# Filler matmuls in the attention layer of a two-layer kernel: out of the loop bodies, and one in each vacant side slot of the last body

## The reference, cut to what matters

```python
# x: (16, 512, 128) float32; 16 heads of 8
x = L0_attn_x
xn = _layernorm(x)
q, k, v = heads(xn, Wq, bq), heads(xn, Wk, bk), heads(xn, Wv, bv)
attn = softmax(q @ k.T * scale * (0.5 + 0.5 * resolve_level))
s = (attn @ v) @ Wp.T + bp
g = _silu(ffn(xn))              # silu(xn @ wg.T) * (xn @ wu.T), then @ wd.T
x = x + s * g                   # layer 0, the one that the change touches
xn = _layernorm(x)
x = x + long_convolution(xn) * _silu(top2_experts(xn))   # layer 1
```

## Time and profile before

| | |
|---|---|
| three timed runs, median (lowest, highest) | 1589.7 us (1583.72 to 1591.99) |
| the profiled execution: time | 1592.2 us |
| the profiled execution: span, first to last instruction | 1590.4 us |
| mean granted TensorE clock | 0.924 |
| PE, DVE, ACT, POOL busy, share of the span | 82%, 65%, 55%, 35% |
| layer 0's last values matmuls end | 1010.1 us |
| a loop body | 58.2 us |

### The profile page before, as it was taken

One profiled execution on the slowest core, in us unless ns is written; L12 is line 12 of the kernel. 1 busy time (PEld: TensorE's weight loads), 2 busy tenths in 40 slices (PEclk: granted clock), 3 DMA queues, 4 the chain that ended last, 5 costly groups with the idle time before them and its releaser, 6 DMA issues. The chain is left out here.

```text
span 1590.4 us, 30375 instructions
## 1 busy us (share of the span) xinstructions
PE 1304.3 (82%) x8202; PEld 676.7 (43%) x8202; DVE 1031.1 (65%) x2496; ACT 869.9 (55%) x1682; POOL 553.7 (35%) x543
## 2 busy tenths in 40 slices
PE   5888998998998998998998898364676389999970
PEld 2433433433433333333343332133343278888860
DVE  1777877877877877877877781054556345545447
ACT  0277776776777777777676775212233144444432
POOL 2122232232232332332332221236555434445440
PEclk9999999999999999999999997555888789999995
DMA  6322202212212212211221300026988422222229
GB/s 225 105 71 107 103 33 88 102 52 67 102 53 66 102 53 70 98 57 66 100 82 39 107 11 13 13 76 229 283 271 269 146 61 68 67 67 69 67 59 317
DMA packets 109858, 160.12 MB, mean 101 GB/s; under 512 B 17489, under 2 KB 47761, under 8 KB 109394
## 3 DMA queue, kind: packets, MB, share of 16 engines
q1 hardware_dynamic: 100242, 141.14, 27.7%
q0 software_dynamic: 8448, 17.58, 3.2%
q10 hardware_dynamic: 1088, 0.54, 0.1%
HBM read 104.20 MB, written 49.77 MB: 97 GB/s over the span
## 5 line engine op out<-in xcount | busy, mean ns | idle before, releaser
L447 DVE TENSOR_REDUCE row_max<-ps_max 128x2 f32<-128x1024 f32 x512 | 623.0, 1221 | 187.5 <-PE ps_max L632 185.0
L599 ACT ACTIVATE probs<-ps_exp 128x512 f32<-128x512 f32 x1024 | 559.1, 602 | 266.2 <-PE ps_exp L632 260.5
L632 PE MATMUL ps_exp<-q_op,k_op 32*128 32x512 f32 x1024 | 320.3, 503 | 22.3 <-ACT probs L599 22.3
L632 PEld LDWEIGHTS ps_exp<-q_op,k_op 32*128 32x128 f32 x1024 | 139.2, 184 | 366.1 <-ACT probs L599 302.8
L712 PE MATMUL ps_y<-probs,v_aug 128*32 128x512 f32 x2048 | 279.7, 619 | 1.2 <-ACT probs L599 1.2
L632 PE MATMUL ps_max<-k_op,q_op 32*128 32x512 f32 x1024 | 253.0, 495 | 2.9 <-DMA k_op<-k_parts_scratch 2.2
L1475 ACT ACTIVATE hidden<-ps_h,b 128x256 f32<-128x256 f32 x268 | 118.6, 473 | 148.1 <-PE ps_h L1452 148.1
L1518 POOL DMA_INDIRECT y_scratch<-result,goes_to x134 | 128.3, 958 | 144.8 <-DVE result L1503 128.4
L1371 POOL DMA_INDIRECT sorted_scratch<-rows,place x128 | 123.5, 965 | 106.8 <-DVE place L1279 69.8
L351 POOL TENSOR_TENSOR rstd<-var_eps,minus_half 128x4 f32<-128x4 f32 x32 | 32.4, 1013 | 318.3 <-DVE var_eps L442 318.3
L1459 PE MATMUL ps_o<-w,hidden 128*128 128x128 f32 x1072 | 132.2, 277 | 0.0
(11 more groups left out here) (160 smaller groups left out, 1471.3 us busy)
## 6 DMA issues: line engine op xcount, KB each, us to landing
toep<-k_pad_scratch SPq DMA_DIRECT2D x32, 1024.0 KB
q_op<-q_parts_scratch SPq DMA_DIRECT2D x16, 1024.0 KB, 5.7
k_op<-k_parts_scratch SPq DMA_DIRECT2D x16, 1024.0 KB, 8.5
unit_rows<-sorted_scratch SPq DMA_DIRECT2D x136, 66.0 KB
q_parts_scratch<-q_hi SPq DMA_DIRECT2D x16, 512.0 KB, 3.1
k_parts_scratch<-k_hi SPq DMA_DIRECT2D x16, 512.0 KB, 2.8
q_parts_scratch<-q_lo SPq DMA_DIRECT2D x16, 256.0 KB, 2.4
k_parts_scratch<-k_lo SPq DMA_DIRECT2D x16, 256.0 KB, 2.1
```

What stands on the lines that cost most here:

```text
L447: dve.tensor_reduce(row_max[group // 2][:, t, head:head + 2], ps_max[u][:, :, :], AX.X, ALU.max)\
L599: act.activation(probs[s % 2][:, i, :], ps_exp[i % 2][:, :], ACT.Exp).then_inc(exp_done, 1)
L632: return pe.matmul(out, lhsT, rhs, start=True, stop=True)
```

## The change

`keep_awake` in `to_side` runs only for side pieces of the head (numbers below 15), no longer in the bodies. In step 5, `second_group` is late and two fillers stand ahead of max1 only in body 0, as before; in bodies 1 to 15 the second group comes first, as in all other steps, and max1 has no filler. In body 15 every vacant slot waits for `side_free` and issues one filler.

```diff
                 elif what == "xnT":
-                    keep_awake()
+                    if isinstance(n, int) and n < len(HEAD_SIDE):
+                        keep_awake()
...
                 elif what[0:3] == "max":
-                    keep_awake()
+                    if isinstance(n, int) and n < len(HEAD_SIDE):
+                        keep_awake()
...
-                    if s != SIDE.index("max1"):
+                    late = s == SIDE.index("max1") and is_first(b)
+                    if not late:
                         second_group()
...
                         what = SIDE[s]
-                        if what == "max1":
+                        if what == "max1" and is_first(b):
                             wait(pe, side_free, side(b, s))
                             keep_awake()
+                            keep_awake()
                         to_side(what, b + of(what), par if of(what) % 2 == 0 else 1 - par, side(b, s))
-                    if s == SIDE.index("max1"):
+                    elif not exists(b + 1):
+                        wait(pe, side_free, side(b, s))
+                        keep_awake()
+                    if late:
                         second_group()
```

## The result

Four runs of the changed kernel took 1544.22, 1527.45, 1544.89 and 1543.33 us, median 1543.78. Beside them the kernel before had a median of 1589.03. The ratio on record is 0.9657, 95% interval 0.9598 to 0.9716; the two medians divided give 0.9715, at the upper end of that interval. So the change makes the kernel 2.8 to 3.4% faster. I had forecast 1524 with a range of 1515 to 1546, so the time lies in the range, near its upper end. The profiled execution took 1544.2 us (span 1542.4), against 1592.2 (1590.4) before: 48.0 us of the 66.4 that the sum promised.

The account below looks back on a forecast made before the run. PE was taken as nearly always occupied, in a ring with ACT of scores, exponentials and values. Loop and body 14 (55.3) plus body 15 (11.1) gave 66.4 us off 1592.2: 1525.8, as a median about 1524, range 1515 to 1546.

Parts of the forecast that it names:

- max1: Steps 5 and 6: second group first and two fillers gone give 2.8 us per body, 39.2 us over 14 bodies.
- the sum: Loop and body 14 55.3 us plus body 15 11.1 us, 66.4 us in total off the profiled 1592.2.
- The lower bound, 1.4: At max1, the gain per body from the fillers alone, if the moved group waits as long as before.
- max0: Steps 12 and 13: removing one filler gives 0.75 us per body (bounds 0.3 and 0.8), 11.2 us over 15 bodies.
- xnT: Steps 8 and 9: filler mostly hidden behind ACT's copy; removing it gives 0.35 us per body, 4.9 us over 14.
- The body as a whole: A full body should go from 58.2 to 54.3 us, 3.9 us less.
- Body 15: Last body: max1 1.9 us, slot 0 minus 1.0, other fillers minus 0.5, clock kept 10.7; 11.1 us gained.
- The filler in slot 0: In body 15's slot 0, the new filler waits for DVE's gate and loses 1.0 us.
- this rival: Clock falls inside the loop behind max1 and max0; 29 slow steps eat 66 us, three per body about 1625; chance 0.06.
- Behind layer 0 nothing changes: After layer 0, no gain or loss; PE idles so long for DMAs that the clock is down again.
- the second rival: ACT, DVE or a DMA takes the gain back in the loop, still faster: 1555; chance 0.2.
- the middle way: Within the rival of gain taken back by ACT, DVE or a DMA: max1 gives 2.1 us per body, time 1540.

Follow-up runs that it names:

- a2_no_last: Changed kernel without the fillers of body 15; ratio to the kernel before 0.9701.
- b3_max1_fill_only: Kernel before without the two fillers at max1 in bodies 1 to 15, old order kept; ratio 0.9934.
- c2_shift: Changed kernel with 96 semaphore-counting instructions ahead of PE's program; ratio to the kernel before 0.9643.
- d2_shift32: Changed kernel with 32 semaphore-counting instructions ahead of PE's program; median 1532.31 us, ratio to the kernel before 0.9579.
- c1_late_load: Changed kernel with body 13's q and k loads started two steps later; ratio to the kernel before 0.9593.
- d1_best: Changed kernel with body 13's q and k loads two steps later and no filler in slot 0 of body 15; median 1527.62 us, ratio to the kernel before 0.9573.
- b0_again: Kernel before, run once more unchanged; one run, 1596.55 us, experts' loop 273.6 us.
- d3_every_other: Changed kernel with fillers only in the even vacant slots of body 15 (7 of 14); ratio to the kernel before 0.9593.
- b4_xnT_max0: Kernel before without the fillers at xnT and max0 in the bodies; ratio 0.9912.

## Why the prediction was right, and where its sum was off

- **max1** is the term as argued: 2.70 per body for 2.8, and singly the order gives 1.5 and the fillers 1.3. The lower bound, 1.4, took the moved group to find a new wait; it finds none.
- **max0 and xnT**: 0.63 for 0.75, and 0.54 for 0.35. I had put the filler at xnT down as mostly hidden behind `y_raw`; more of it counted.
- **The body as a whole**: 3.62 for 3.9. The sites add up to 3.87, but 0.25 is lost in three other intervals, which my sum had as unchanged. Over bodies 1 to 12 the shortfall is 3.5 us.
- **Body 15**: from the last values matmuls of body 14 to the end of layer 0 it took 63.5 us before (946.56 to 1010.1) and 50.8 after (902.60 to 953.4), so 12.7 gained for 11.1. The filler in slot 0 does wait for DVE's gate. That step, values to values, takes 3.73 us in place of 3.18, so it costs 0.55 and not 1.0. The other steps take 3.08 to 3.15 us with a filler in each and the clock at 1.00, where vacant steps of the kernel before took 3.09: the fillers cost nothing there. Against a body 15 of the new order without fillers (a2_no_last) they are worth 16.2 us; the prediction's 11 counted only what the kernel before had lost, which fell later.

The body's first slots in the timeline of the changed kernel, against the earlier trace rows:

```profile
904.31 0.69 DVE L468 SCALAR_TENSOR_TENSOR gate<-tanh_z,ps_side 128x512 f32<-128x512 f32 x1 [0.30 <-ACT tanh_z L583]
905.05 0.91 PE L632 MATMUL ps_side<-wu,wg 128*128 128x384 f32 x2 [0.71 <-DVE gate L468]
...
927.16 0.89 PE L632 MATMUL ps_exp<-q_op,k_op 32*128 32x512 f32 x2
...
929.40 0.91 PE L632 MATMUL ps_side<-wu,wg 128*128 128x384 f32 x2
...
930.25 0.89 PE L632 MATMUL ps_exp<-q_op,k_op 32*128 32x512 f32 x2
...
952.31 1.06 PE L714 MATMUL ps_y<-probs,v_aug 128*32 128x512 f32 x8 [0.33 <-ACT probs L599]
```

- **The clock in the loop** held at 1.00 without the 59 fillers, but for the 6.8 us behind the stall. The prediction weighed against that what the Trainium skill, TensorE: Matmul & The Clock Gate, Part 4 (PE-mode transpose), says, that transposes do not count as PE activity like matmuls. The runs do not refute it: in the old order the slot of transposes with an idle time on either side did let the clock fall (b3_max1_fill_only), and between score groups without idle time it did not. I gave this rival 0.06. It did not come true here, but my walk gave no reason why the new order should keep the clock, and with the old one the loss is real: a fall costs a body 1.5 to 2.7 us (58.4 to 59.6 against 56.93).
- **What failed**: "Behind layer 0 nothing changes", and a loop that ends without cost. The 20 us between 1524 and 1544 are 18.4 in the profiled execution. Lost are 6.0 at the stall on leaving the loop, 0.3, 3.5 and 1.2 in body 0, bodies 1 to 12 and body 13, and 12.1 in the experts' loop. Regained are 1.3 in the head and bodies 14 and 15 together, 3.2 between layer 0 and the experts and 0.2 behind them. That makes 18.4.
- **The stall**: that it is PE's code arriving late is shown by moving the code (gone in c2_shift and d2_shift32) and by moving the loads (1.8 and 1.5 us). The 1.2 us of body 13 belong to it. From the v slot to g0 this body takes 4.94 us where those of the loop take 3.73, since the v slot runs at half clock; in c2_shift, d2_shift32, c1_late_load and d1_best, where the clock didn't fall, it is 3.72 or 3.73. So the stall costs 7.2 us in all. ACT idles 1.40 us in step 6 of that body (at 816.60), with scores ready. But that is no loss of the change: the kernel before idles as long in the same step, 1.63 us, and the interval from max1 to g2 shrinks there by 6.77 - 3.92 = 2.85 us, as forecast. What ACT waits for is open. The wait in the kernel before:

```profile
856.62 1.08 ACT L599 ACTIVATE probs<-ps_exp 128x512 f32<-128x512 f32 x2 [1.63 <-PE ps_y L712]
```

- **The experts' loop**: that its 12.1 us are chance is only made likely (b0_again), not shown.
- **The range**: its upper end, 1546, was set for waits in the loop that would take the gain back. The time lies under it, but what took it there are mostly a stall and a slower experts' loop, both of which the prediction had at nothing. That 1543.8 is inside is in part luck.
- **Slips in the working**, none of which moves the forecast: the middle way of the second rival is 1589.7 - (14 x 2.1 + 4.5 + 11) = 1545, not 1540. And a step at half clock does take 4.55 us, but that is read from the timeline (values matmuls at 970.50 and 975.05), not from the 30 records in 9.5 us. The head has 16 side pieces, so the condition of the change holds for numbers below 16.
- With the stall gone, the difference of medians on one chip is 1598.3 - 1532.3 = 66.0 us (d2_shift32). This agrees with the 66.4 of the sum, but layer 0 gained 65.0 us there only with the shorter head, and what happens behind layer 0 varies by more than the difference.

The best version is the change with body 13's loads two steps later (d1_best, 0.9573) or with PE's code shifted (d2_shift32, 0.9579); their intervals overlap, so neither is shown to be the better one. The later loads are the more robust edit, as they don't hang on where the code lies.

## What to carry to other kernels

A filler that holds the clock should be priced together with the order around it: here two fillers stood where PE idled on both sides, and issuing the next group first made them needless, gave ACT its work 2.5 us earlier, and was worth slightly more (1.5 us per body) than the fillers themselves (1.3). Put fillers where the engine really runs dry (the last body), and no more than fit into the idle time of a step. After a change to a tuned loop, look at its exit: here the code behind the hardware loop had to be fetched, and large loads issued just then delayed it. And a digit of a page's clock line is a mean over its slice, so look at the clock in stretches before calling it full.

## What the hardware showed that I had not expected

- PE stopped 4.5 to 5.3 us in the middle of a group of matmuls, at the first straight-line body behind a hardware loop, while one 16 KB instruction packet arrived among loads that kept the DMA engines fully busy. It was there in every profile of the changed kernel and of the two (a2_no_last, d3_every_other) that differ from it in body 15 alone, 2.4 us in b4_xnT_max0, 1.5 to 1.8 us with later loads, and gone when 32 or 96 instructions stood ahead of the program. Half clock followed for 6.8 us after the stalls of 2.4 us and more, and not after those of 1.5 and 1.8.
- 96 more instructions at the start delayed the first v slot by 3.9 us (42.78 against 38.85), 32 by nothing (38.34).
- The clock fell and came back within 3.4 to 6.8 us in the loop with old order and no filler, but stayed at 0.50 for the rest of the layer in body 15 without fillers (a2_no_last).
- The experts' loop takes 259 to 278 us in one and the same code; this is more than the 0.5% by which I had judged what a measurement can tell.
